# Splitting six weight pieces early and keeping them in DRAM, and making the similarities before the stage ends: one decoder layer on one Trainium2 core

## The chip, the cores and the metric

The kernel runs on one core of one Trainium2 chip. The metric is the device time of one execution in microseconds; the time given for a kernel is the median of several executions. All data are fp32, and every product of matrices is made of three passes over a "high" and a "low" part of each operand (float32r), so each weight and each activation is split into two parts before TensorE (PE) may use it.

## The reference

There are 32 batches of 128 positions by 1024 features. Three blocks follow each other, each with a residual and a layer norm:

```python
x = _layernorm(x + attention(x, wq, wk, wv, wo))       # 32 heads, 8 KV heads, rope, causal
x = _layernorm(x + xattn(x, ctx, weight))              # conv over 3 taps, inputs scaled by att
x = _layernorm(x + ffn(x, A, B, Wr, br))               # rank 16, 8 routed experts

def xattn(feature, embedding, weight):                 # embedding = ctx, [32, 128, 1024]
    # cosine of each column of the embedding with its left neighbour, itself, its right one
    sim = stack([cos(embedding, emb_l), cos(embedding, embedding), cos(embedding, emb_r)], 1)
    att = repeat(sim, C, axis=1)                       # [32, 3 * 128, 1024]
    out = einsum('bit,oi->bot', unfold3(feature) * att, weight)
```

With 128 positions the choice of key chunks leaves every key allowed, so the attention is a plain causal one. The three "similarities" of a batch depend on ctx alone.

## The kernel before, in words

**Stage one** (`part1`) runs steps t = 0 to 33. Step t projects batch t to q, k and v on PE (72 matmuls of 128x512, `project`, L483), and works on the attention of batch a = t-1 in eight chunks p = 0 to 7. A chunk goes from PE scores (`score`, L513) to DVE (`mask_min`), ACT (`exponent`, L769), DVE (`invert`, L629), POOL (`scale`, L915), DVE (`turn_p`, L637), and then by DMA (`move_p`, L322: ten small DMAs for each half of a batch) to `weigh` (L526). ACT copies the turned queries to SBUF (`copy_q`, L756) before `score` may run. The result goes to DRAM (`ot_dram`). Beside this each step squares and sums ctx (`square`, `neighbour`), stores the sums in DRAM (`cs_dram`), loads the next x (`load_x`, L297) and makes its high part at chunk 2 (`high_x`, L742).

Each engine has a written order of its own. The steps are a hardware loop with a few steps unrolled before it (LEAD) and after it (TAIL). Engines meet only by semaphores, and SP issues nearly all DMAs, in order, on one queue.

**Hand-over.** Stage two needs other weights in the same SBUF region: eight pieces of `wo`, `wb` and `wx`, ten "late pieces" in all. Each is loaded to a landing buffer, its high part is made by ACT (`high_later`, L796) and its low part by DVE (L644) or POOL (L928). Pieces 0 to 3 are made in step 31, the last projecting step, 4 to 8 in step 32 and `wb` in step 33. In step 32 PE has no projection; it does the output projection of batch 0 (`project_out`, L543) between the last scores, in step 33 that of half of batch 1. ACT also makes the high part of the attention output of batch 1 (`high_out(1)`, L827). The cosines come from the sums: `load_sums` and a lower bound (L725) in step 32, then a square root on ACT (L821), a reciprocal (L671) and four products on DVE, and the stores `store_sims` to `sim_dram` in step 33. SP then waits for these stores and loads half of the factors `att` of batch 0 (`start_att`, L985 and L990). At the end of the stage all engines meet at a barrier (L145).

**Stage two** (`part2`) has per step 48 matmuls of the output projection (L1197), 18 of the convolution (L1211), the low-rank block, and on DVE, ACT and POOL the products, norms and splits that feed them. Its first convolution multiplies `att` by the normalised x (`multiply`, L1380); DVE, POOL and ACT make the first norm (`average`, `invert_root`, `normalise1`, L1537). `turn_x2` (L1230) comes after the second norm of batch 0.

Of the kernel before, what the change touches and what calls it, by code (L numbers as in the profile page):

```python
# [23 lines left out]
P = 128  # L24
KT = D // P
HEADS, KVH, DH = 32, 8, 32
NU = 2
# [83 lines left out]
def build(nc, xT, x, ctx_in, wqkv, wo, wx, wa, wb, br, rope, mask, ident, out):  # L111
    ot_dram = nc.dram_tensor("ot_scratch", [B, P, D], F32, kind="Internal").ap()
    cs_dram = nc.dram_tensor("cs_scratch", [B, 2, D], F32, kind="Internal").ap()
    sim_dram = nc.dram_tensor("sim_scratch", [B, len(SIM_TABLE), D + SIM_PAD], F32, kind="Internal").ap()
    with ExitStack() as both:
# [28 lines left out]
            att, [both.enter_context(nc.semaphore(f"att_in{n}")) for n in range(2)])  # L144
        with ExitStack() as ctx:  # L145
            part1(nc, ctx, weights, raw, halves, wo_ps, handoff, xT, ctx_in, wqkv, wo, wx, wb,
                  rope, mask, ident, x, ot_dram, cs_dram, sim_dram)
# [4 lines left out]
def part1(nc, ctx, weights, raw, halves, wo_ps, handoff, xT, ctx_in, wqkv, wo, wx, wb,  # L152
          rope, mask, ident, x, ot_dram, cs_dram, sim_dram):
# [6 lines left out]
    def sem(name):  # L160
# [7 lines left out]
     added0, counted0, y0, stats0, xn1, kept, att, att_in) = handoff  # L168
# [72 lines left out]
    LEAD, TAIL = 4, 4  # L241
# [24 lines left out]
    LATER = KT + 2  # L266
    BY_POOL = (1, 3, 5, 8, 9)
    landing = [raw[:, 1], ctx_t[:, 0:D], raw[:, 0]]

    def lands(n):  # L270
        return n % 3 if n < KT + 1 else 1

    def later_parts(n):

        src = landing[lands(n)]
        if n < KT:
            return [(src, wo_sb[:, 0, n], wo_sb[:, 1, n])]
        if n == KT + 1:
            return [(src, wb_sb[:, 0], wb_sb[:, 1])]
        return [(src[:, 0:TAPS * P], wx_sb[:, 0], wx_sb[:, 1])]  # L280
# [7 lines left out]
    sqs, nbs, norm = nb[:, 0:QD + 1], nb[:, QD + 1:2 * QD + 1], nb[:, 2 * QD + 1:3 * QD + 2]  # L288
    own = rot1[:, 0, 0:QD]
    own_out = sem("own_out")  # L290
    right, ot_last = kept

    @block.sync
    def _(sp):
# [30 lines left out]
        def store_first_half(b):  # L325

            wait(sp, ot_read, after(b, NU, 1))
            sp.dma_start(ot_dram[b, :, 0:BANK], ot[:, 0]).then_inc(ot_out[0], 16)
# [6 lines left out]
        def load_later(n):  # L335
# [10 lines left out]
            dst, arrived = landing[lands(n)], later_in[lands(n)]  # L346
            if n < KT:
                sp.dma_start(dst, wo[:, n, :]).then_inc(arrived, 16)
            elif n == KT + 1:
                sp.dma_start(dst, wb).then_inc(arrived, 16)  # L350
            else:
                sp.dma_start(dst[:, 0:TAPS * P], wx).then_inc(arrived, 16)

        def load_o(t):

            wait(sp, x_lo, 2 * (B - 1 + t))
            if t == 1:
                later_done(sp, KT - 2)
# [4 lines left out]
        def load_third_o():  # L363

            later_done(sp, KT)
# [4 lines left out]
        def load_sums():  # L370

            sums = cs_dram[0, 0, 0:1]
            sp.wait_ge(cs_out, 16 * B)
            sp.wait_ge(summed, B)
            for dst, at, width in ((sqs, 0, QD + 1), (nbs, D, QD)):
                sp.dma_start(dst, bass.AP(tensor=sums.tensor, offset=sums.offset + at,
                                          ap=[[2 * D, B], [QD, 4], [1, width]])).then_inc(cs_in, 16)
# [8 lines left out]
        def store_sims():  # L386

            sp.wait_ge(sim_made, 1)
            for n in (3, 4):
                sp.dma_start(sim_row(sim_dram, n, 0), right).then_inc(sim_out, 16)  # L390
            sp.wait_ge(sim_made, 2)
            sp.dma_start(sim_row(sim_dram, 2, 0), own).then_inc(own_out, 16)
# [14 lines left out]
        def step(t, par):  # L407
# [19 lines left out]
            if at_step(t, LAST):  # L427
                store_sims()
                store_first_half(b)
                sp.wait_ge(own_out, 16)  # L430
                sp.wait_ge(sim_out, 16 * 6)
                start_att(sp, att, att_in, sim_dram, 0, 0)
            if at_step(t, B):
                load_later(7)
                load_later(8)
# [3 lines left out]
                sp.wait_ge(sq_done, B)  # L439
                sp.dma_start(xn1[:], x[1]).then_inc(xn_in[1], 16)  # L440
# [4 lines left out]
            if valid(t):  # L445
# [4 lines left out]
                             csum[:]).then_inc(cs_out, 16)  # L450
            if at_step(t, B - 1):
# [4 lines left out]
            if at_step(t, B):  # L456
                load_later(9)
                load_third_o()
            if at_step(t, B - 2):
# [3 lines left out]
            if at_step(t, B):  # L463
                store_later_half(b)
            if at_step(t, B - 1):
                load_later(4)

        steps(sp, step, 0, LAST, LEAD, TAIL)
        sp.wait_ge(ot_out[0], 16 * B)
        sp.wait_ge(ot_out[1], 16 * (B - 1))  # L470

    @block.tensor
    def _(pe):
# [58 lines left out]
        def project_out(t, n, k):  # L532
# [3 lines left out]
            if t == 0 and n == 0:  # L536
                later_done(pe, k)
# [53 lines left out]
    def _(dve):  # L591
# [76 lines left out]
        def invert_norms():  # L668

            dve.wait_ge(root, 1)  # L670
            dve.reciprocal(norm, norm).then_inc(cos_step, 1)  # L671

        def cosines():

            dve.wait_ge(cos_step, 1)
            dve.tensor_tensor(right, norm[:, 0:QD], norm[:, 1:QD + 1], ALU.mult).then_inc(cos_step, 1)
            dve.tensor_tensor(own, norm[:, 0:QD], norm[:, 0:QD], ALU.mult).then_inc(cos_step, 1)
            dve.wait_ge(cos_step, 2)
            dve.tensor_tensor(right, right, nbs, ALU.mult).then_inc(sim_made, 1)
            dve.wait_ge(cos_step, 3)  # L680
            dve.tensor_tensor(own, own, sqs[:, 0:QD], ALU.mult).then_inc(sim_made, 1)
# [10 lines left out]
        def step(t, par):  # L692
# [5 lines left out]
            for p in range(NC):  # L698
                if p == 0 and valid(a):
                    rotate(a, 1 - par, 2)  # L700
                if p == 0 and valid(b):
                    invert(b, NC - 1)
# [1059 lines left out]
```

## Time and profile before

| | |
|---|---|
| median of 3 executions | 1395.01 us (1394.53 to 1395.64) |
| the profiled execution | 1392.16 us, of which its span from the first to the last instruction is 1390.1 us |
| PE busy | 1355.7 us, 98% of the span |
| DVE, ACT, POOL busy | 79%, 67%, 70% |
| granted TensorE clock | 0.992 of full speed |
| HBM | 131.83 MB read, 34.47 MB written |

Stage one fills about the first 757 us of the span and stage two the rest. A matmul's busy time includes its pipeline, so a busy PE can still be held to less than its peak; idle time is what waits show directly. A late piece is a tile `weights<-raw` or `weights<-ctx_t` in the trace.

### The profile page before, as it was taken

What the parts mean: (1) busy time and instruction counts of PE and PEld (TensorE: products, weight loads), DVE (VectorE), ACT (ScalarE), POOL (GpSimd) and SP (SyncE); (2) the same over time, 40 slices, a digit from 0 to 9 for tenths busy, and PEclk for the clock granted to TensorE, in tenths of its full rate; (3) what the DMA queues carried; (4) which work ended last, traced back from release to release, by engine and by line L of the source; (5) the groups of instructions that cost most, each with busy time, mean ns of one, the idle gap of its engine ahead of it and who ended that gap; (6) DMA issues with size and microseconds to landing.
All of it is one profiled execution on the core that took longest, in us unless ns stands there. A gap on an engine that the chain in (4) does not pass through costs nothing. (4 is left out here: it accounts for less than half of the span.)

```text
span 1390.1 us, 32350 instructions
## 1 busy us (share of the span) xinstructions
PE 1355.7 (98%) x8306; PEld 1056.5 (76%) x8306; DVE 1095.9 (79%) x3873; ACT 927.2 (67%) x3262; POOL 979.0 (70%) x932
## 2 busy tenths in 40 slices
PE   8999999999999999999986999999999999999996
PEld 6777777777777777777764788888888888888884
DVE  6877787878778777878785688878887788877877
ACT  5887878878888887878785455545554455545544
POOL 4877777777777776777775677667776677767762
PEclk9999999999999999999998999999999999999999
DMA  7354545445453545445468866676665766666652
GB/s 266 100 160 116 159 116 161 121 146 149 121 161 115 165 115 152 132 134 159 131 201 242 185 159 166 157 174 153 161 156 164 172 152 165 156 169 157 161 122 76
DMA packets 109005, 213.03 MB, mean 153 GB/s; under 512 B 26656, under 2 KB 32288, under 8 KB 108960
## 3 DMA queue, kind: packets, MB, share of 16 engines
q1 hardware_dynamic: 108336, 211.46, 56.5%
q10 hardware_dynamic: 624, 1.05, 0.2%
q8 instruction: 18, 0.29, 0.1%
q14 instruction: 27, 0.22, 0.1%
HBM read 131.83 MB, written 34.47 MB: 120 GB/s over the span
## 5 line engine op out<-in xcount | busy, mean ns | idle before, releaser
L483 PE MATMUL wo_ps<-weights,halves 128*128 128x512 f32 x2304 | 569.7, 399 | 3.0 <-DVE weights L685 2.9
L483 PEld LDWEIGHTS wo_ps<-weights,halves 128*128 128x128 f32 x2304 | 421.5, 188 | 138.0 <-issue 53.3
L769 ACT ACTIVATE pexp<-sm,smin 128x128 f32<-128x128 f32 x1024 | 398.1, 391 | 100.6 <-DVE smin L622 99.7
L1197 PE MATMUL wo_ps<-weights,halves 128*128 128x512 f32 x1464 | 368.2, 399 | 4.3 <-PEq L145 4.3
L915 POOL TENSOR_TENSOR pn<-pexp,prec 128x512 f32<-128x512 f32 x256 | 266.7, 1047 | 98.5 <-DVE prec L629 98.5
L1667 POOL TENSOR_TENSOR prods<-prod,prods 128x512 fp32r<-128x512 f32 x186 | 251.6, 1360 | 119.9 <-ACT prods L1528 114.9
L1197 PEld LDWEIGHTS wo_ps<-weights,halves 128*128 128x128 f32 x1464 | 270.3, 189 | 62.6 <-issue 5.2
L622 DVE CUSTOM_DVE_ANT_0 sm<-s_ps,mask_t 128x128 f32<-128x128 f32 x1024 | 231.9, 282 | 26.1 <-PE s_ps L513 20.9
L1528 ACT CAST prods<-prod 128x512 fp32r<-128x512 f32 x189 | 117.1, 620 | 181.0 <-DVE prod L1380 146.7
L769 ACT ACTIVATION_READ_ACCUMULATOR pexp<-sm,smin 128x1 f32 x1024 | 193.0, 189 | 0.0
L1380 DVE TENSOR_TENSOR prod<-att,x 128x512 f32<-128x512 f32 x189 | 185.1, 993 | 9.5 <-DMA att<-sim_scratch 7.2
L637 DVE STREAM_TRANSPOSE blocks<-pn 128x512 f32<-128x512 f32 x256 | 178.0, 695 | 6.5 <-POOL pn L915 6.2
L1211 PE MATMUL conv_ps<-prods,weights 128*128 128x512 f32 x567 | 144.2, 396 | 1.7 <-POOL prods L1667 1.2
L910 POOL TENSOR_TENSOR xn<-rot,y 128x512 f32<-128x512 f32 x64 | 83.8, 1310 | 68.5 <-DVE y L609 68.3
L1356 DVE BATCH_NORM_STATS2 stats<-y 128x6 f32<-128x512 f32 x188 | 127.3, 690 | 4.4
L1211 PEld LDWEIGHTS conv_ps<-prods,weights 128*128 128x128 f32 x567 | 105.9, 188 | 28.6 <-POOL prods L1667 2.6
L1661 POOL TENSOR_TENSOR moments<-moments,power 128x1 f32<-128x1 f32 x96 | 76.7, 799 | 62.7 <-DVE moments L1365 62.7
L629 DVE RECIPROCAL prec<-psum_row 128x4 f32<-128x4 f32 x256 | 44.9, 175 | 67.5 <-ACT pexp L769 67.5
L889 POOL TENSOR_TENSOR halves<-raw,halves 128x512 fp32r<-128x512 f32 x62 | 79.7, 1287 | 25.1 <-ACT halves L742 25.1
L604 DVE TENSOR_TENSOR rot<-wo_ps,rope_t 128x512 f32<-128x512 f32 (+1 forms) x96 | 56.7, 591 | 44.0 <-PE wo_ps L483 42.1
L1653 POOL TENSOR_TENSOR halves<-raw,halves 128x512 fp32r<-128x512 f32 x60 | 90.6, 1510 | 0.0
L622 DVE DVE_READ_ACCUMULATOR2_ANT smin<- 128x1 f32 x1024 | 85.1, 83 | 0.0
(130 smaller groups left out, 1645.8 us busy)
## 6 DMA issues: line engine op xcount, KB each, us to landing
att<-sim_scratch SPq DMA_DIRECT2D x192, 252.0 KB
pt<-blocks SPq DMA_DIRECT2D x636, 64.0 KB, 2.0
ctx_t<-in_ctx SPq DMA_DIRECT2D x32, 576.0 KB, 5.1
raw<-in_xT SPq DMA_DIRECT2D x32, 512.0 KB, 3.8
xn<-in_x SPq DMA_DIRECT2D x32, 512.0 KB, 7.6
ot_scratch<-ot SPq DMA_DIRECT2D x63, 256.0 KB, 2.1
raw<-ot_scratch SPq DMA_DIRECT2D x31, 512.0 KB, 6.8
out<-late SPq DMA_DIRECT2D x31, 512.0 KB, 6.2
```

Source lines behind the costliest of these rows:

```text
L483: mm = pe.matmul(qkv_ps[(par + g) % 2][:], xs[:, par, xl, k], w_sb[:, wl, g, k], start=(k == 0 and n == 0), stop=(k == KT - 1 and n == 2))
L622: ins = dve.tensor_tensor_reduce(sm[:, c % 2, i * P:(i + 1) * P], s_ps[i][:, j * P:(j + 1) * P], mask_t[:], 1.0, 3e38, ALU.add, ALU.min, s ...
L637: dve.transpose(blocks[:, u, :, j], pn[:, c % 2].rearrange("p (i b k) -> p b i k", i=NI, b=QB)).then_inc(turned, 1)
L769: ins = nc.scalar.activation(pexp[:, c % 2, i * P:(i + 1) * P], sm[:, c % 2, i * P:(i + 1) * P], ACT.Exp, bias=smin[:, c % 2, i:i + 1], sc ...
L915: pool.tensor_tensor(pn[:, c % 2].rearrange("p (i s) -> p i s", i=NI), pexp[:, c % 2].rearrange("p (i s) -> p i s", i=NI), prec[:, c % 2]. ...
L1197: mm = pe.matmul(wo_ps[n][:], os_t[:, par, ol, k], wo_sb[:, wl, k, n * BANK:(n + 1) * BANK], start=(k == 0 and m == 0), stop=(k == KT - 1 ...
L1211: mm = pe.matmul(conv_ps[h][:], wx_sb[:, wl, k], prods_home(t, m, xl), start=(k == 0 and n == 0), stop=(k == TAPS - 1 and n == 2))
L1356: dve.bn_stats(stats[own][:, half], src).then_inc(counted[n], 1)
L1380: dve.tensor_tensor(prod_home(t, m), att[:, k, h * BANK:(h + 1) * BANK], x1[:, par, h * BANK + k:h * BANK + k + BANK], ALU.mult).then_inc( ...
L1528: nc.scalar.copy(prods_home(t, m, 0), prod_home(t, m)).then_inc(prod_hi, 1)
L1653: pool.tensor_tensor(lo, oraw[:, par, cols], hi.bitcast(F32), ALU.subtract).then_inc(o_lo, 1)
L1667: pool.tensor_tensor(prods[:, m % PB, 1], prod[:, m % PB], prods[:, m % PB, 0].bitcast(F32), ALU.subtract).then_inc(prod_lo, 1)
```

## The change

Six of the ten late pieces (wo pieces 4 to 7, `wb` and `wx`) are no longer made in steps 32 and 33. In steps 2 to 7 SP loads one of them a step into `att`, which stage one does not otherwise use; ACT makes the high part at chunk 5 and POOL the low part (128x1024) at chunk 6, and at the start of the next step SP stores both parts to a new DRAM buffer. They come back to their places in the weight region as 1 MB DMAs: pieces 0 and 1 at the end of step 31, 2 and 3 at the start of step 32, `wb` and `wx` later in step 32. Only pieces 0 to 3 of `wo` are still made at the end.

The similarities of batches 0 to 15 are made in steps 20 to 25 with 64 partitions (each small operation at chunk 5), and `att` of batch 0 is loaded whole in steps 26 to 29, one of its four DMAs at the end of each step, ahead of the next step's `load_x`. Those of batches 16 to 31 are made at the end. The first norm of batch 0 is made before the barrier, and also the two parts of the attention output of batch 2. `high_out(1)` moves from chunk 6 to chunk 5 of step 32. `xn1` is loaded at the end of step 31. The unrolled ends grow from 4 and 4 steps to 10 and 14.

```diff
-    LEAD, TAIL = 4, 4
+    LEAD, TAIL = 10, 14
+    FIRST = B // 2
+    EARLY = B - 12
...
-    LATER = KT + 2
-    BY_POOL = (1, 3, 5, 8, 9)
+    LATER = KT // 2
+    BY_POOL = (1, 3)
+    SPLIT_AT = 2
+    SPLITS = KT // 2 + 2
...
+        def load_source(n):
+            wait(sp, split_lo, n)
+            sp.dma_start(split_parts(n)[0], split_source(n)).then_inc(split_src, 16)
+        def store_split(n):
+            sp.wait_ge(split_lo, n + 1)
+            both = split_parts(n)[1]
+            sp.dma_start(split_dram[n, :, :, 0:both.shape[2]], both).then_inc(split_out, 16)
+        def load_split(n):
+            sp.wait_ge(split_out, 16 * SPLITS)
+            sp.wait_ge(qkv_done, after(B - 1, NG, 2 if n < SPLITS - 2 else NG))
+            home = split_home(n).bitcast(F32)
+            sp.dma_start(home, split_dram[n, :, :, 0:home.shape[2]]).then_inc(split_in[n], 16)
...  (SP's step: at its start)
+            if at_step(t, EARLY):
+                load_sums(False)
+            for n in range(SPLITS):
+                if at_step(t, SPLIT_AT + n + 1):
+                    store_split(n)
+                if at_step(t, SPLIT_AT + n):
+                    load_source(n)
             if at_step(t, B):
-                load_sums()
-                load_later(5)
-                load_later(6)
+                load_sums(True)
+                load_split(2)
+                load_split(3)
...
             if at_step(t, LAST):
-                store_sims()
                 store_first_half(b)
-                sp.wait_ge(own_out, 16)
-                sp.wait_ge(sim_out, 16 * 6)
-                start_att(sp, att, att_in, sim_dram, 0, 0)
+                store_sims(True)
             if at_step(t, B):
-                load_later(7)
-                load_later(8)
                 load_o(1)
...  (and at its end)
+            for n in range(len(RUNS) + 1):
+                if at_step(t, EARLY + 6 + n):
+                    ...
+                    start_att(sp, att, att_in[0], sim_dram, 0, 0, D, (n,))
             if at_step(t, B - 1):
-                load_later(4)
+                load_split(0)
+                load_split(1)
+                sp.dma_start(xn1[:], x[1]).then_inc(xn_in[1], 16)
...  (ACT)
+        def high_split(n):
+            src, both = split_parts(n)
+            act.wait_ge(split_src, 16 * (n + 1))
+            wait(act, split_out, 16 * n)
+            nc.scalar.copy(both[:, 0].bitcast(F32R), src).then_inc(split_hi, 1)
...  (DVE)
             if at_step(t, LAST):
-                invert_norms()
-                cosines()
                 add_first(1)
+                average_first()
+                invert_norms(True, 0, HALF_QD)
+                invert_norms(True, HALF_QD, QD + 1)
+                pair_norms(True)
+                cosines(True)
+                low_third_out()
```

## Rows read from the trace of the kernel before

**Rows 1.** Busy time by stretch: us, PE, PEld, DVE, ACT, POOL, clock, DMA share, GB/s.
```profile
0.00:20.00 20.00, 15.76 (x47) 10.72 (x48) 11.18 (x12) 12.81 (x12) 3.55 (x9) 0.91 0.92 344
...
40.00:620.00 580.00, 579.32 (x4239) 430.76 (x4240) 463.98 (x2301) 476.66 (x2259) 429.64 (x394) 1.00 0.48 139
...
720.00:740.00 20.00, 15.56 (x126) 9.88 (x127) 17.58 (x74) 16.16 (x63) 12.96 (x9) 0.91 0.80 248
740.00:760.00 20.00, 12.67 (x55) 7.69 (x54) 9.72 (x28) 8.91 (x26) 8.89 (x7) 0.91 0.91 259
760.00:800.00 40.00, 37.21 (x159) 29.66 (x160) 25.13 (x51) 18.63 (x26) 26.50 (x26) 0.92 0.90 189
```

**Rows 2.** Timeline of PE, hand-over: start, duration, [idle before it <- what ended it].
```profile
746.63 1.94 PE L526 MATMUL pv_ps<-pt,v_t 128*32 128x512 f32 x8 [3.17 <-DMA pt<-blocks]
...
755.24 1.06 PE L526 MATMUL pv_ps<-pt,v_t 128*32 128x512 f32 x8 [0.47 <-DMA pt<-blocks]
760.62 7.88 PE L1197 MATMUL wo_ps<-weights,halves 128*128 128x512 f32 x21 [4.31 <-PEq L145]
...
777.61 5.64 PE L1197 MATMUL wo_ps<-weights,halves 128*128 128x512 f32 x24
784.36 1.06 PE L1230 MATMUL ffn_ps<-id_t,late 128*128 128x128 f32 x8 [1.11 <-ACT late L1547]
```

**Rows 3.** Timeline of SP's queue, steps 32 and 33.
```profile
736.19 0.33 SPq L361 DMA_DIRECT2D raw<-ot_scratch  x1
...
750.97 1.53 SPq L390 DMA_DIRECT2D sim_scratch<-kept  x2
...
759.05 0.77 SPq L990 DMA_DIRECT2D att<-sim_scratch  x1
```

**Rows 4.** Timelines of ACT and DVE, steps 32 and 33.
```profile
742.03 1.04 ACT L827 CAST halves<-raw 128x1024 fp32r<-128x1024 f32 x1
...
745.11 1.28 ACT L821 ACT_TABLE_LOAD   x1
746.40 0.42 ACT L821 ACTIVATE nb<-nb 128x257 f32<-128x257 f32 x1
...
756.37 0.59 ACT L778 COPY kept<-pv_ps 128x512 f32<-128x512 f32 x1 [2.87 <-PE pv_ps L526]
...
747.09 1.72 DVE L671 RECIPROCAL nb<-nb 128x257 f32<-128x257 f32 x1
```

**Rows 5.** Timelines of SP, ACT, POOL and PE in one steady step.
```profile
653.92 0.36 SPq L297 DMA_DIRECT2D raw<-in_xT  x1
...
646.20 0.40 ACT L769 ACTIVATE pexp<-sm,smin 128x128 f32<-128x128 f32 x1 [2.13 <-DVE smin L622]
...
655.57 0.39 ACT L769 ACTIVATE pexp<-sm,smin 128x128 f32<-128x128 f32 x1
...
657.96 1.05 ACT L742 CAST halves<-raw 128x1024 fp32r<-128x1024 f32 x1 [0.75 <-DMA raw<-in_xT]
...
660.47 0.56 ACT L756 COPY qt<-turn_ps 128x512 f32<-128x512 f32 x1
...
653.46 1.05 POOL L915 TENSOR_TENSOR pn<-pexp,prec 128x512 f32<-128x512 f32 x1
...
661.79 1.17 PE L513 MATMUL s_ps<-kt,qt 32*128 32x128 f32 x32
```

**Rows 6.** Timelines of POOL and DVE: low parts of late pieces.
```profile
719.85 3.37 POOL L928 TENSOR_TENSOR weights<-raw,weights 128x1024 fp32r<-128x1024 f32 x1
...
731.63 2.42 POOL L928 TENSOR_TENSOR weights<-raw,weights 128x1024 fp32r<-128x1024 f32 x1
...
719.29 1.68 DVE L644 TENSOR_TENSOR weights<-raw,weights 128x1024 fp32r<-128x1024 f32 x1
```

**Rows 7.** Issue to landing of v_t<-v_new (L309): step 28, then step 30.
```profile
DMA to landing us min/median/max: 5.4/5.4/5.4
...
DMA to landing us min/median/max: 7.5/7.5/7.5
```

More of the change, by code:

```diff
@@ L287, in part1, with sim_parts @@
     QD = D // 4
-    sqs, nbs, norm = nb[:, 0:QD + 1], nb[:, QD + 1:2 * QD + 1], nb[:, 2 * QD + 1:3 * QD + 2]
-    own = rot1[:, 0, 0:QD]
-    own_out = sem("own_out")
+    HALF_QD = QD // 2
     right, ot_last = kept
+    ot_first = xn0[:, BANK:D]
+    def sim_parts(late):
+        rows = slice(4 * FIRST, P) if late else slice(0, 4 * FIRST)
+        flat = nb if late else att[:].rearrange("p k d -> p (k d)")
+        sums, mults, norm = (flat[rows, n * (QD + 1):n * (QD + 1) + width]
+                             for n, width in enumerate((QD + 1, QD, QD + 1)))
+        pair = (right[rows, :], xn0[rows, 0:QD]) if late else (
+            flat[rows, 3 * (QD + 1):3 * (QD + 1) + QD], flat[rows, 4 * (QD + 1):4 * (QD + 1) + QD])
+        return sums, mults, norm, *pair
     @block.sync
@@ L384, in store_zeros, with store_sims @@
                              allow_slow_non_contiguous=True).then_inc(sim_out, 16)
[L386 to L392, printed above, removed]
+        def store_sims(late):
+            first, count = (FIRST, B - FIRST) if late else (0, FIRST)
+            to_right, to_own = sim_parts(late)[3:5]
+            sp.wait_ge(sim_made, 2 * late + 1)
+            for n, shift in ((0, 1), (1, 1), (3, 0), (4, 0)):
+                sp.dma_start(sim_row(sim_dram, n, shift, first, count), to_right).then_inc(sim_out, 16)
+            sp.wait_ge(sim_made, 2 * late + 2)
+            sp.dma_start(sim_row(sim_dram, 2, 0, first, count), to_own).then_inc(own_out, 16)
         sp.dma_start(xraw[:, 0], xT[0]).then_inc(x_in[0], 16)
@@ L666, in add_first, with low_third_out @@
             dve.bn_stats(stats0[:, half], y0[:, cols]).then_inc(counted0, 1)
-        def invert_norms():
-            dve.wait_ge(root, 1)
-            dve.reciprocal(norm, norm).then_inc(cos_step, 1)
[L673 to L681, printed above, removed]
+        def low_third_out():
+            dve.wait_ge(o_hi, 3)
+            hi, lo = (halves[:, 0, part].rearrange("p t s -> p (t s)") for part in range(2))
+            dve.tensor_tensor(lo, raw[:, 0], hi.bitcast(F32), ALU.subtract).then_inc(o_lo, 2)
@@ L775, in read_ot @@
             wait(act, pv_done, after(a, NU, u + 1))
-            if not (at_step(a, B - 1) and u == 1):
-                wait(act, ot_out[u], after(a, 16, 0))
-            nc.scalar.copy(ot_last if at_step(a, B - 1) and u == 1 else ot[:, u], pv_ps[:]).then_inc(ot_read, 1)
+            if at_step(a, B - 1):
+                if u == 0:
+                    act.wait_ge(added0, 2)
+                nc.scalar.copy((ot_first, ot_last)[u], pv_ps[:]).then_inc(ot_read, 1)
+                return
+            wait(act, ot_out[u], after(a, 16, 0))
+            nc.scalar.copy(ot[:, u], pv_ps[:]).then_inc(ot_read, 1)
         def move_last_row():
@@ L993, in sim_row, with start_att @@
-def sim_row(sim_dram, n, shift):
-    row = sim_dram[0, n, 0:1]
+def start_att(sp, att, arrived, sim_dram, t, lo, hi, parts=range(len(RUNS) + 1)):
+    cols, width = slice(lo, hi), hi - lo
+    for n in parts:
+        if n < len(RUNS):
+            (first, last), row = RUNS[n], (0, 2, 3)[n]
+            sp.dma_start(att[first:last, :, cols],
+                         sim_dram[t, row, cols].unsqueeze(0).unsqueeze(0).broadcast_to([last - first, TAPS, width])
+                         ).then_inc(arrived, 16)
+        else:
+            rows = sim_dram[t, 0:TAPS, cols]
+            both_edges = bass.AP(tensor=rows.tensor, offset=rows.offset,
+                                 ap=[[2 * (D + SIM_PAD), 2]] + [list(d) for d in rows.ap])
+            sp.dma_start(att[EDGES[0]:EDGES[1] + 1:EDGES[1] - EDGES[0], :, cols], both_edges).then_inc(arrived, 16)
@@ L1077, in part2 @@
     held = sem("held2")
[L1078 removed]
+    shifted = [first_steps[3]] + [sem(f"shifted{n}") for n in range(1, 3)]
     stored = [sem("stored0"), sem("stored1")]
@@ L1439, in step @@
                 low_lt(z)
-            if valid(c):
+            if valid(c) and not at_step(c, 0):
                 average(c, 0)
```

235 lines of the change are left out of this document (143 added, 92 removed).

## The prediction

> **What bounds the kernel now.** I read the busy time by stretch first [rows 1]. From 40 to 620 us PE is busy 579.32 of 580 us: in the steady part of stage one nothing can be won by unloading DVE, ACT or POOL, and everything that makes PE wait is lost. From 720 to 760 us PE is busy for only 28.2 of 40 us, and from 760 to 800 for 37.2 of 40. The hand-over is the only place with something to win, and most of the change's work is there. ACT is busy 82% and POOL 74% in the steady part; what the change puts there has to fit in their holes.
>
> Then PE's own timeline [rows 2]. In step 33 PE waits 3.17 us, and later 0.47 us, for the DMAs that bring the last probabilities; then comes the barrier, 4.31 us; then 21 matmuls take 7.88 us where the same kind runs at 24 in 5.64 us a little later (so 21 would take 4.9): the granted clock is at its lower level, 1.2 instead of 2.4 GHz, for part of them. The last wait is 1.11 us for the second norm of batch 0. After this PE is full again, so any time gained up to 784.36 us is kept.
>
> Third, who comes last to the barrier. PE ends at 755.24 + 1.06 = 756.3 us, ACT's last copy at 756.37 + 0.59 = 757.0 [rows 4], and SP's last issue, the loads of `att`, at 759.05 + 0.77 = 759.8 [rows 3]. PE starts 0.8 us after that. SP sets the barrier, not PE.
>
> **The barrier.** The change takes the `att` loads and the wait for the sims' stores off SP's end. What SP has left is the first-half store and five stores of sims, at 1.53 / 2 = 0.77 us each for four and some 0.6 for the fifth [rows 3]. They need the cosines. The last transposes end as the old reciprocal begins, at 747.1 [rows 4]; from there DVE does the second half of the first sum with its statistics (some 1.4 us, an estimate), the average (0.5), two reciprocals (1.72 together) and four small products (1.6, an estimate from their size): 752.3. SP can then end at 752.3 + 3.1 + 0.6 = 756.0. `low_third_out` is a 128x1024 subtract, 1.7 us on DVE [rows 6], done by 754.0. So ACT's copy at 757.0 is now last, and PE starts at about 757.0 + 0.8 = 757.8 instead of 760.6: **-2.9 us**, if the last probabilities land when they did.
>
> **Do they land earlier?** ACT loses five casts in step 32 (four at 1.04, one at 0.5), 4.7 us [rows 4]; DVE and POOL lose as much. One would hope for up to 4.7 us. But `high_out(1)` now stands one chunk earlier, and ACT blocks there until the attention output of batch 1 has landed. SP can issue that load some 3 us earlier than at 736.19 [rows 3], since it no longer waits for the splits of two pieces. Ahead of it are, from 720.7 on, four split pieces of 1.05 MB, `xn1` 0.52, sums 0.26, v 0.13, the ten DMAs of one half of the probabilities, 0.66 in all, and one store of 0.26: 6.0 MB. The stretch with the largest DMAs moved 344 GB/s at a share of 0.92, so 374 at a full share [rows 1]: 16 us, and 1.4 for the load itself, with some 2 us around them: 740.2. After the cast follow two chunks (four exps of 0.39 each, 1.6) and one copy (0.5): the table load would start at 744.9, against 745.11 [rows 4]. So ACT's gain is eaten by the queue, and the end of step 33 stays where it was. Bounds: at 420 GB/s, 1.9 us less; at 259, the rate of 740 to 760 us [rows 1], the load lands after 747, and the end is 5 to 6 us later. I take **0**.
>
> **After the barrier.** `att` is in SBUF, the first norm is made, and ACT and POOL have no split of batch 2 in front of them. Convolutions still come at fixed places in PE's order, behind 21 matmuls. Nothing is won if these are as slow as now and the chain to `turn_x2` keeps its length; at most the 2.9 us of the clock and the 1.11 us of the wait, 4.0 [rows 2]. PE was at the low level after the idle times of 3.17 and 4.31 us: 1.94 us for eight matmuls of L526 against 1.06. The gap at the barrier shrinks to 1.4 us, but before the last `weigh` a gap of about 3 us opens, because the projection ahead of it ends earlier while the DMAs do not. So the lower half is likelier: **-1.7 us**.
>
> **Steps 2 to 7.** ACT's cast is 1.04 us; at chunk 5 ACT has a hole of 2.13 us [rows 5], and the piece, queued behind x, ctx and one 1 MB store, lands some 9 us after the step's first load, before ACT is there. POOL's low part is 2.42 us, or 3.37 where DVE read two SBUF operands at the same time (its own low part, 719.29) [rows 6]; DVE has no such instruction in these steps, so 2.42. It delays `scale` of the last chunk from 653.46 to 655.9; the second exp chunk of the next batch, which waits for it, starts at 656.9 instead of 655.57 and ends at 658.4, where `high_x` starts at 657.96 because of its DMA: 0.45 late. `copy_q` ends at 661.5 instead of 661.0, and `score` is due at 661.79 [rows 5]: hidden, with 0.3 us left. At 3.37 it would be 0.7 a step. **+0.1.** Two more DMAs a step on SP cost under 1 us of issue, in front of loads with 9 us of slack. Should that cover be gone, six steps times the 0.7 would be 4 us.
>
> **Steps 20 to 25.** The early root makes ACT load a table twice: 1.28 + 0.42 + 1.28 = 2.98 us [rows 4] in the same 2.13 us hole; 0.85 late, most of which the margin before the next `score` takes: **+0.3**. The DVE pieces (0.4 to 0.9 us each) fit before the rotation for which it waits. SP's five stores, 3.7 us, stand in its idle time before `move_p`.
> The Trainium skill, "ScalarE: Activation LUTs", section "What ACT_TABLE_LOAD costs", puts a switch at some 2.66 us, drain included: 5.7 us here, and +3.0 instead of +0.3. The trace differs: the root starts 0.01 us after the load ends.
>
> **Steps 26 to 29.** Three DMAs of 504 KB for `att` (42 partitions, three rows of 4 KB each) stand right ahead of `load_x`; the fourth is small. ACT already waits 0.75 us for x in each step, so all delay of x goes through. The queue is in order: with a load of 512 KB put before it in step 30, v_t landed in 7.5 us instead of 5.4 [rows 7]. So x comes later by 0.4 of issue and by 1.0 (504 KB at full rate, half hidden by the store ahead) to 2.1 us. From `copy_q`'s end at 661.03 to `score` at 661.79 there are 0.76 us [rows 5]. PE waits 0.6 to 1.7 us a step; the next step hangs on PE's time, so it repeats: 1.9 to 5.2 in three steps. I take 0.93 each, **+2.8 us**.
>
> **Sum.** -2.9 + 0 - 1.7 + 0.1 + 0.3 + 2.8 = -1.4 us on the profiled execution of 1392.16 us (2.1 us of which lie outside its span): 1390.8. The median is 2.85 us above that execution, so 1393.6. About 2.8 us, 0.2%, is what a measurement of this kernel can tell from no change. The gain at the barrier is half given back in steps 26 to 28.
>
> **Rivals.** (1) *It pays.* x is held up by no more than the margin (PE waits 0.3 a step, not 0.93), and PE starts stage two at 2.4 GHz: -2.9 - 4.0 + 0.1 + 0.3 + 0.9 = -5.6, **1389.4**; with a faster queue another 1.9. For it: the `att` DMAs may overlap x's; against it: rows 7 and the gap before `weigh`. 0.37.
> (2) *The queue is flooded* in step 32, the rival on the other side. At 259 GB/s the 6 MB need 23 us, and ACT's cast of batch 1 starts at 748 instead of 742.03; exps, transposes, last probabilities and the barrier follow, 5 to 6 us later: -1.4 + 5.5 = +4.1, **1399.1**. It turns to a loss once that load lands after about 743.5. For it: small DMAs lie between the large ones; against it: all of the large ones have rows of 4 KB, as in the stretch with 344 GB/s. 0.12.
> (3) *`att` is slow to load*: while such loads ran, the queues moved 189 GB/s at a share of 0.90 [rows 1], where 504 KB take 2.7 us. PE then waits 2.2 us in each of three steps, 3.9 more than in the sum: -1.4 + 3.9 = +2.5, **1397.5**; with the 0.4 us that the rows leave open it is beyond 0.2%, and I count it as slower. 0.10.
> (4) *The table switch costs more*: if each of the two loads in step 20 held ACT for its own length again (1.28) [rows 4], `copy_q` would come 2.6 us later and PE wait all of it: -1.4 + 2.6 = +1.2, **1396.2**. The root directly behind its load speaks against it. 0.03. The Trainium skill's "ScalarE: Activation LUTs" is the page by whose figure it would be so.
> (5) The forecast, within 0.2% of before: 0.38.
>
> **How the numbers follow.** Faster 0.37 (rival 1), same 0.41 (forecast and rival 4), slower 0.22 (rivals 2 and 3). The likeliest case's own range is 1392.2 to 1396.5. The range for 8 in 10 leaves out the best of rival 1 and the worst of rival 2: 1388.5 to 1399.
>
> **What would show it.** The wait of PE at the barrier should fall from 4.3 to about 1.4 us, and its first matmul of stage two come at about 761 (757.8 plus 3.2 of delays in stage one). `high_x` should wait for x 2 to 3 us, not 0.75, in steps 27 to 29, each with a new wait of PE for `copy_q` of about 1 us, and none in steps 2 to 7. The table load at the end of step 32 should keep its distance to the step's start, with ACT waiting at `high_out(1)` for its DMA. The forecast is wrong if that wait is absent (then rival 1 with the faster queue), if it is over 5 us (rival 2), or if PE shows waits for `copy_q` in the six splitting steps.

## The result, and the profile after

The changed kernel takes **1414.79 us** (median of 4 executions, 1411.68 to 1417.62) against 1395.33 for the kernel before beside it: ratio 1.0136, 95% interval 1.0115 to 1.0157. It is 19.5 us slower, where 1393.6 was forecast and 1399 was the upper end. The profiled execution took 1411.68 us; its span is 1409.9 us against 1390.1.

Busy time by stretch, changed kernel (us, PE, PEld, DVE, ACT, POOL, clock, DMA share, GB/s):

```profile
40.00:620.00 580.00, 572.78 (x4172) 424.60 (x4171) 461.60 (x2284) 478.53 (x2247) 437.30 (x395) 1.00 0.55 152
620.00:720.00 100.00, 91.98 (x654) 67.83 (x653) 71.37 (x359) 73.58 (x351) 66.34 (x61) 0.98 0.56 146
720.00:740.00 20.00, 17.69 (x112) 13.13 (x114) 15.67 (x67) 16.36 (x57) 15.25 (x13) 0.91 0.60 184
740.00:760.00 20.00, 12.47 (x117) 8.41 (x111) 12.14 (x73) 11.61 (x55) 10.72 (x9) 0.91 1.01 331
```

From 40 to 620 us PE was idle for 0.68 us before [rows 1] and is idle for 7.2 now; in the next 100 us it is idle for 8.0, against 2.8 before. The time went in the steady part, where nothing of PE's own work was touched. PE's waits over the whole changed kernel (total us, times, longest):

```profile
PE s_ps L576 <- ACT qt L860: 13.5, 13, 3.8
PE pv_ps L589 <- DMA pt<-blocks: 12.9, 3, 8.4
...
PE wo_ps L1328 <- PEq L151: 0.9, 1, 0.9
```

Before, these three were 4.2 us (3 times), 3.6 and 4.3. `score` waits for `copy_q` thirteen times, the last probabilities cost three times as much, and the barrier, as forecast, almost nothing. PE's timeline in the hand-over shows the last two and the low clock behind them:

```profile
761.17 1.93 PE L589 MATMUL pv_ps<-pt,v_t 128*32 128x512 f32 x8 [8.41 <-DMA pt<-blocks]
769.49 1.06 PE L589 MATMUL pv_ps<-pt,v_t 128*32 128x512 f32 x8 [1.02 <-DMA pt<-blocks]
779.66 1.19 PE L589 MATMUL pv_ps<-pt,v_t 128*32 128x512 f32 x8 [3.42 <-DMA pt<-blocks]
781.80 7.60 PE L1328 MATMUL wo_ps<-weights,halves 128*128 128x512 f32 x21 [0.94 <-PEq L151]
...
804.54 1.06 PE L1361 MATMUL ffn_ps<-id_t,late 128*128 128x128 f32 x8 [1.10 <-ACT late L1680]
```

Set against [rows 2]: 3.17 has become 8.41 us, the barrier's 4.31 has become 0.94, and 21 matmuls take 7.60 instead of 7.88.

To place the rest I noted, in PE's timeline, when the first transposition of `turn_k` starts in each step (steps are numbered by SP; `turn_k(31)` is the last). The table gives these starts, then the first matmul of stage two, `turn_x2`, and the span, for the kernels of this study. A steady step is 22.24 us long.

| us | before | changed | unrolled only | att moved | queue order | x early | all three | half pieces |
|---|---|---|---|---|---|---|---|---|
| `turn_k(0)` | 23.69 | 25.64 | 24.12 | | | 24.34 | 24.17 | |
| `turn_k(9)` | 221.71 | 226.71 | 223.01 | | | 221.48 | 221.38 | |
| `turn_k(26)` | 600.04 | 608.87 | 605.58 | | | 600.95 | 600.85 | |
| `turn_k(31)` | 711.34 | 730.09 | 717.76 | 718.25 | 731.35 | 712.45 | 712.35 | 714.05 |
| stage two | 760.62 | 781.80 | 767.87 | 771.21 | 780.50 | 763.12 | 763.14 | 760.18 |
| `turn_x2` | 784.36 | 804.54 | 791.50 | 794.13 | 802.26 | 785.29 | 784.92 | 781.82 |
| span | 1390.1 | 1409.9 | 1397.6 | 1399.5 | 1407.6 | 1390.6 | 1390.3 | 1387.1 |

The changed kernel's 19.8 us of span, read down the column: 1.95 before `turn_k(0)` (the first x landed later and a POOL subtract took 3.5 instead of 2.5 us; this stretch varies from 23.7 to 25.6 us over the runs, whatever the edit); 6.9 up to `turn_k(26)`; 9.9 from there to `turn_k(31)`, the steps with the `att` loads (11.2 and 13.4 in the traces of runs 4 and 3 below, which load `att` at the same place); 2.4 in the hand-over (51.71 us from `turn_k(31)` to stage two instead of 49.28); -1.0 up to `turn_x2`; -0.4 after.

One of the `att` steps shows the whole chain, in the timelines of SP, ACT and PE:

```profile
659.61 7.29 SPq L355 DMA_DIRECT2D pt<-blocks  x10
666.94 0.58 SPq L363 DMA_DIRECT2D ot_scratch<-ot  x1
667.57 0.44 SPq L1114 DMA_DIRECT2D att<-sim_scratch  x1
668.05 0.39 SPq L330 DMA_DIRECT2D raw<-in_xT  x1
...
675.31 1.04 ACT L846 CAST halves<-raw 128x1024 fp32r<-128x1024 f32 x1 [5.48 <-DMA raw<-in_xT]
...
677.81 0.56 ACT L860 COPY qt<-turn_ps 128x512 f32<-128x512 f32 x1
...
678.43 2.09 PE L576 MATMUL s_ps<-kt,qt 32*128 32x128 f32 x32 [3.77 <-ACT qt L860]
```

The load of x stands behind ten small DMAs, a store and an `att` load. It lands 7.2 us after its issue (3.8 is the median in the kernel before); ACT sits idle for 5.48 us, `copy_q` is queued behind the cast, `score` comes 3.77 us late and then runs at the lower granted clock, 1.2 instead of 2.4 GHz (32 matmuls in 2.09 instead of 1.17 us). In the four steps PE waits 1.98, 1.67, 3.77 and 0.60 us.

The hand-over, from SP's queue in steps 31 and 32:

```profile
739.45 1.26 SPq L399 DMA_DIRECT2D weights<-split_scratch  x2
740.76 0.60 SPq L528 DMA_DIRECT2D xn<-in_x  x1
741.45 1.23 SPq L425 DMA_DIRECT2D nb<-cs_scratch  x2
742.78 1.28 SPq L399 DMA_DIRECT2D weights<-split_scratch  x2
...
752.42 1.60 SPq L408 DMA_DIRECT2D raw<-ot_scratch  x1
```

The attention output of batch 1 (L408) lands 11.7 us after its issue, and in ACT's timeline `high_out(1)` waits for it, with the exps, the table load and the last copies behind it:

```profile
764.19 1.04 ACT L939 CAST halves<-raw 128x1024 fp32r<-128x1024 f32 x1 [7.97 <-DMA raw<-ot_scratch]
...
768.82 1.28 ACT L930 ACT_TABLE_LOAD   x1
...
780.90 0.58 ACT L883 COPY kept<-pv_ps 128x512 f32<-128x512 f32 x1 [4.27 <-PE pv_ps L589]
```

### The profile page after: what moved, and what is told of

It is laid out like the page before. It is cut to its first block and busy times, and to the rows that moved or that the text cites. A ratio compares the mean times of both kernels' runs of the same rounds, so it can differ in the third digit from the quotient of the medians.

```text
span 1409.9 us, 31220 instructions
## 1 busy us (share of the span) xinstructions
PE 1360.6 (97%) x8306; PEld 1059.6 (75%) x8306; DVE 1096.1 (78%) x3878; ACT 929.1 (66%) x3265; POOL 985.2 (70%) x934
## 5 line engine op out<-in xcount | busy, mean ns | idle before, releaser
L1001 POOL TENSOR_TENSOR halves<-raw,halves 128x512 fp32r<-128x512 f32 x62 | 80.7, 1302 | 45.6 <-ACT halves L846 45.5
L576 PEld LDWEIGHTS s_ps<-kt,qt 32*128 32x128 f32 x2048 | 63.8, 188 | 39.0 <-ACT qt L860 20.9
L576 PE MATMUL s_ps<-kt,qt 32*128 32x128 f32 x2048 | 76.0, 285 | 14.7 <-ACT qt L860 13.5
```

The costliest lines, as they stand in the source:

```text
L576: mm = pe.matmul(s_ps[i][:, j * P:(j + 1) * P], qt[rows, u, j * P:(j + 1) * P], kt[rows, par, u * P:(u + 1) * P], start=True, stop=True, t ...
```

## Experiments

My first theory after the result was that four things had been added: the longer straight-line ends of the loops, the `att` loads ahead of x, the flooded queue of step 32, and perhaps the split work of ACT and POOL in steps 2 to 7. Rivals were that one of them was all of it, and that the split work was what cost in the early steps. Medians are given beside the ratio to the kernel before in the same session.

**1. Unrolling alone.** The kernel before, one line changed:

```diff
-    LEAD, TAIL = 4, 4
+    LEAD, TAIL = 10, 14
```

> The kernel before with only the unrolled ends grown from 4 and 4 steps to 10 and 14. The changed kernel lost 18.8 us in stage one (turn_k of step 31 at 730.09 us instead of 711.34) before the hand-over began. Theory A (the losses are x arriving late behind new DMAs): unrolling costs nothing, 1394 to 1397 us, no new wait of PE in steps 0 to 29. Theory B (more straight-line code, so more instruction fetches beside the data, slows everything a little; in the changed kernel x lands in 4.3 to 4.9 us even in steps without new DMAs, against 3.8): 2 to 6 us slower, x landing at 4.3 us or more.

Measured 1400.93 us, ratio 1.0043 (1.0027 to 1.0060): some 6 us for no new work, and x lands 4.4 us (median) after its issue instead of 3.8. That is theory B. Where the time goes, in the timelines of SP, ACT and PE:

```profile
516.52 7.89 SPq L322 DMA_DIRECT2D pt<-blocks  x10
524.45 0.59 SPq L328 DMA_DIRECT2D ot_scratch<-ot  x1
525.08 0.46 SPq L297 DMA_DIRECT2D raw<-in_xT  x1
...
529.88 1.05 ACT L742 CAST halves<-raw 128x1024 fp32r<-128x1024 f32 x1 [3.13 <-DMA raw<-in_xT]
...
533.00 1.17 PE L513 MATMUL s_ps<-kt,qt 32*128 32x128 f32 x32 [1.41 <-ACT qt L756]
...
360.12 6.25 SPq L322 DMA_DIRECT2D pt<-blocks  x10
```

Once the loop has gone round once, SP issues the ten DMAs of the probabilities in about 6.2 us, each time. In the unrolled steps, and in the loop's first pass, one issue in every step or two takes 0.9 to 1.9 instead of 0.6 us, and x, which comes behind, is late by more than the 0.76 us that `copy_q` has in hand [rows 5]. From 30 to 700 us there are 22 issues of 0.9 us or more in this trace, 31 in the changed kernel's and 6 before, none of them in a later pass of the loop. PE's waits for `copy_q` sum to 5.2 us up to 715 us (9 times), against 0.6 before.

**2. The `att` loads moved** behind the store of the context sums, some 10 us ahead of the next x:

```diff
+            for n in range(len(RUNS) + 1):
+                if at_step(t, EARLY + 6 + n):
+                    ...
+                    start_att(sp, att, att_in[0], sim_dram, 0, 0, D, (n,))
             if at_step(t, B - 1):
                 load_later(2)
```

(the same lines go from the step's end)

> The changed kernel with one move: in steps 26 to 29 the DMA for att is issued behind the store of the sums, some 10 us before the next x, instead of right ahead of load_x. Theory A (att in front of x costs the 10 us of steps 27 to 30): 9 to 10 us faster than the changed kernel, 1404 to 1406 us, and steps 27 to 30 at 22.3 us each. Rival (the load from sim_dram itself is slow and disturbs wherever it stands): less than 4 us faster, 1411 us or more.

Measured 1401.17 us, ratio 1.0048 (1.0033 to 1.0063): 12 to 14 us faster than the changed kernel, more than theory A's 9 to 10, and the four steps are 22.31 to 22.44 us long. In the traces the steps from `turn_k(26)` to `turn_k(31)` give 9.5 us of it (111.7 instead of 121.2); the rest I can't place. The `att` loads cost what they do by where they stand.

**3. The queue of step 32** in another order:

```diff
                 load_sums(True)
-                load_split(2)
-                load_split(3)
...
                 load_o(1)
                 wait(sp, q_turned, NU * B)
                 sp.dma_start(xn0[:], x[0]).then_inc(xn_in[0], 16)
+                load_split(2)
+                load_split(3)
+                sp.wait_ge(sq_done, B)
+                sp.dma_start(xn1[:], x[1]).then_inc(xn_in[1], 16)
```

(`xn1` is no longer loaded at the end of step 31)

> The changed kernel with another order of the large loads in steps 31 and 32: xn1, and pieces 2 and 3, behind the first ten probability DMAs of step 32, the load of the attention output of batch 1 and xn0. Theory A (the flood: 4.7 MB ahead of the probabilities make PE wait 8.4 us and ACT 8.0 us): these two waits fall below 3 us and the hand-over shortens by 3 to 6 us, 1409 to 1412 us. Rival (the bytes count, not their order; a later transfer then waits as long): the same time within 1.5 us, with the wait at another DMA.

Measured 1409.4 us, ratio 1.0107 (1.0089 to 1.0124): about 4 to 5 us faster, though this interval and the changed kernel's (1.0115 to 1.0157) overlap. From `turn_k(31)` to stage two it takes 49.15 us instead of 51.71. The waits for the last probabilities fall from 12.9 to 2.9 us, but PE waits 3.9 us for a split piece instead. The time is in theory A's range; that the wait moves to another DMA is what the rival said.

**4. The split work left out.** Pieces 1 to 5 are neither loaded, cast nor subtracted in steps 3 to 7; their stores stay, with the data of piece 0. The computation is changed by that.

```diff
-            sp.wait_ge(split_lo, n + 1)
+            sp.wait_ge(split_lo, 1)
-                    if p == 5 and at_step(t, SPLIT_AT + n):
+                    if n == 0 and p == 5 and at_step(t, SPLIT_AT + n):
                         high_split(n)
```

(and the same condition before `load_source` and `low_split`)

> The changed kernel with the loads, casts and subtracts of pieces 1 to 5 left out in steps 3 to 7 (their parts are those of piece 0, so part of the computation is left out); the six 1 MB stores stay. The changed kernel loses 3.4 us between steps 2 and 9. Theory A (POOL's 2.4 us delays the next exp and with it copy_q): 2.5 to 3.5 us faster than the changed kernel, 1411 to 1412.5 us, and no wait of PE in steps 4 to 8. Rival (the 1 MB stores make x late): the waits stay, within 1 us of the changed kernel.

Measured 1411.9 us, ratio 1.0120 (1.0103 to 1.0136). The median is in theory A's range, but the interval overlaps the changed kernel's, and the trace speaks for the rival: from `turn_k(0)` to `turn_k(9)` it takes 200.5 us against 201.1, and steps of 22.9 to 23.4 us are still there. By the trace the split work of ACT and POOL costs next to nothing; runs 5 and 6 settle it.

**5 to 8. One edit against all the losses of stage one.** If all of it is x coming late, x has only to be asked for earlier: its buffer is free from the step before on.

```diff
             if valid(t + 1):
-                if not at_step(t, 0) and not at_step(t, 1) and not at_step(t, 2):
-                    load_x(t + 1, 1 - par)
                 load_ctx(t + 1)
...
                 wait(sp, pv_done, after(a - 1, NU, 1))
-            if at_step(t, 1):
-                load_x(3, 1)
+            if valid(t + 2) and not at_step(t, 0):
+                load_x(t + 2, par)
```

It was made in the unrolled kernel of run 1, in the changed kernel, and in the changed kernel with edits 2 and 3, which also ran without it.

> The kernel before with its ends unrolled to 10 and 14 steps (1400.93 us, 5.9 over before), and in every step the load of x for the step after the next now stands before the store of the context sums, some 10 us earlier than at the start of the next step. Theory A: unrolling costs because single DMA issues of SP take 1.2 to 1.9 us in straight-line code, and x, issued last of the chain, comes later than the 0.76 us that copy_q has in hand; with x some 10 us early the same slow issues stay but PE's waits for copy_q in unrolled steps vanish, and the time is 1395 to 1396.5. Rival B: what costs is the slow issues in front of the ten DMAs of the probabilities, or slow instructions of PE itself; then x early changes nothing, 1400 to 1401.5, or worse, since x's 512 KB are now in front of the probabilities.

> The changed kernel with nothing different but the loads of x, issued some 10 us earlier as in the run above; the loads of att in steps 26 to 29 stand where the change has them. Theory A: att costs its 10 to 13 us through x alone, so steps 27 to 30 fall from 24.34, 24.03, 27.59 and 22.96 us to about 22.3, and with the losses of the other unrolled steps gone too the time is 1414.8 - 10 - 5 = about 1399 to 1401 us. Rival B: att's DMAs delay the context, v and the probabilities just as much; then PE waits there instead and the time stays above 1406 us.

> The changed kernel with both earlier edits: the att loads behind the store of the context sums (alone 1401.17 us) and, in step 32, xn1 and two split pieces behind the attention output of batch 1 (alone 1409.4 us). Theory A: the two faults are separate and add: 1401.2 - 5.4 = 1395.8 us. Rival B: they share their loss, because the later start of step 32 let the queue run empty or the split pieces are missed by the output projection (3.9 us of wait in the run of that edit alone) whatever comes before: 1398 to 1400 us.

> The run above and x early in every step as well: the change with its three faults mended. Theory A: 1395.8 less about 5 us of unrolled steps = 1391 us, so that the gain at the barrier is seen in the time. Rival B: with 1400 from the run above and x early worth nothing: 1398 to 1400 us.

| kernel | without x early | with x early |
|---|---|---|
| before, unrolled | 1.0043 (1.0027 to 1.0060) | 1394.37 us, 1.0004 (0.9994 to 1.0013) |
| changed | 1.0136 (1.0115 to 1.0157) | 1393.92 us, 0.9998 (0.9988 to 1.0008) |
| changed, att and queue moved | 1399.4 us, 1.0031 (1.0019 to 1.0044) | 1392.07 us, 0.9985 (0.9975 to 0.9995) |

Theory A holds for these three runs (5, 6 and 8), for 5 and 8 to about 1 us; in run 6 I had still left 5 us too much, since more than the unrolled steps' and the `att` loads' losses came back. The slow issues are all still there (22 in run 5, 33 in run 6, counted as in run 1), and so is each `att` load. The same step of run 6, on SP and ACT:

```profile
647.91 7.33 SPq L355 DMA_DIRECT2D pt<-blocks  x10
655.28 0.58 SPq L363 DMA_DIRECT2D ot_scratch<-ot  x1
655.90 0.45 SPq L1112 DMA_DIRECT2D att<-sim_scratch  x1
656.45 0.34 SPq L336 DMA_DIRECT2D ctx_t<-in_ctx  x1
...
658.03 1.03 ACT L844 CAST halves<-raw 128x1024 fp32r<-128x1024 f32 x1
```

The ten issues again take over 7 us and `att` is ahead of ctx, but ACT casts x at its turn, with no wait, and the steps are 22.30 us long. PE's one wait from 200 to 700 us is then this, against 9.2 us for `copy_q` in the changed kernel:

```profile
PE turn_ps L563 <- ACT kt L863: 0.8, 1, 0.8
```

It stands in step 20, the early root. Run 7's time is in rival B's range (1399.4, where A gave 1395.8), but the trace does not bear out B's cause. From `turn_k(31)` to `turn_x2` it takes 72.8 us instead of run 2's 75.9, so the new queue gains 3.1 us there, as it gained 3.5 in run 3 (70.9 against 74.5); the wait for a split piece, 4.1 us, was in run 3 too (3.9). What is longer is `turn_k(0)` to `turn_k(9)`, 202.5 us against run 2's 200.2, where the two kernels do the same: x coming late costs more in one execution than in another. By the ratios the repairs would add to 1.0048 - 0.0029 = 1.0019, the edge of run 7's interval. Whether they add is open.

**9. The control.** The kernel before with x early, the same diff.

> The kernel before with nothing different but x loaded some 10 us earlier: the control for the runs with x early (1394.4, 1393.9 and 1392.1 us). Theory A: before loses to late x only what its few unrolled steps lose; PE's steps of over 22.24 us there sum to some 0.3 to 0.7 us, so it gains at most that, 1394.3 to 1395 us, and the run with all three edits stays 1.5 to 2.5 us faster. Rival B: x early is worth 1.5 us or more in any kernel, 1392 to 1393 us, and then the change is worth nothing even when mended.

Measured 1393.05 us, ratio 0.9987 (0.9978 to 0.9996), 1.8 us. That is B's forecast. The trace shows 0.5 us of it (`turn_k(31)` at 711.38 in spite of a start 0.56 later, all steps of 22.86 and 22.35 us gone); for the rest I have no row, and the interval allows it to be noise. So the mended change (0.9985) is not shown to be faster than the kernel before with the same mend.

**10. Another order of step 32:** all three edits, and

```diff
+                load_split(2)
...
                 load_o(1)
+                load_split(3)
                 wait(sp, q_turned, NU * B)
                 sp.dma_start(xn0[:], x[0]).then_inc(xn_in[0], 16)
-                load_split(2)
-                load_split(3)
```

> The run with all three edits (1392.07 us), with the queue of step 32 in another order: one split piece where the change has it, then the attention output of batch 1, then the second split piece, xn0 and xn1. There PE waited 4.6 us for the second or first split piece and 3.0 us for the last probabilities. Theory A: the piece that PE waits for lands some 3 us earlier and the attention output at most 2 us later, so that the two waits together fall by 2 to 4 us: 1388.5 to 1390.5. Rival B: the bytes ahead of the last probabilities are the same, and one wait takes over what the other gives: 1391.5 to 1393.

Measured 1392.37 us, ratio 0.9979 (0.9969 to 0.9989); run 8 was at 0.9985. By the time that is B; the two intervals overlap. It is the fastest version that computes everything, 2 to 3 us better than the kernel before, and not told apart from run 9. Its profiled execution was its slowest (1396.76 us), with no wait for a split piece and 12.5 us of waits for the probabilities, so that trace shows one wait taking over from the other, but not in a typical execution: the hand-over differs by some us from one to the next.

**11 and 12. Whose straight-line code is it?** Again the kernel before; in 11 all engines but SP have the long ends, in 12 only SP has them:

```diff
         steps(sp, step, 0, LAST, 4, 4)      # run 11, with LEAD, TAIL = 10, 14
         steps(sp, step, 0, LAST, 10, 14)    # run 12, with LEAD, TAIL = 4, 4
```

> The kernel before with the program ends of PE, DVE, ACT and POOL unrolled to 10 and 14 steps, and SP's left at 4 and 4. With all five unrolled it took 1400.93 us, 5.9 over before. Theory A: the slow issues of SP come from SP's own straight-line program; looped, it issues evenly and the loss is gone, 1395 to 1396 us. Rival B: they come from the fetching of all engines' instructions, which shares the queues with the data; then most of the loss stays, 1398.5 to 1401 us.

> The reverse: the kernel before with only SP's program unrolled to 10 and 14 steps. Theory A: nearly the whole loss comes back, 1399 to 1401 us, with PE's waits for copy_q in unrolled steps. Rival B: under 1.5 us of it, 1395 to 1396.5 us.

Measured 1400.92 us, ratio 1.0036 (1.0024 to 1.0048), for run 11, and 1396.32 us, ratio 1.0002 (0.9993 to 1.0011), for run 12. Theory A, which I held, falls: SP's slow issues come although SP's own program is looped (17 of them; the group of ten at 516.02 us takes 7.48 us), and are no more than before when only SP is unrolled (7, against 6). PE's waits for `copy_q` up to 715 us are 6.1 us in run 11 and 2.2 in run 12. What goes with the slow issues is the instruction traffic of the others, in the table of DMA queues up to 720 us (packets, MB, share), run 11 and then run 12:

```profile
q8 instruction: 30, 0.49, 0.3%
q14 instruction: 45, 0.37, 0.2%
```

```profile
q8 instruction: 9, 0.15, 0.1%
q14 instruction: 20, 0.16, 0.1%
```

Run 1 has 30 and 49 packets there, before has 9 and 16. The Trainium skill, "DMA: Bandwidth & Descriptors", section "Queues, rings and completion order", has queue row 14 as the runtime's own, for refills among others; the trace's name for q14, "instruction", fits that. That the packets themselves hold up SP's issue, and not something else in those engines' programs, is argued, not shown.

**13 and 14. Where the barrier's 3 us went.** With x early the changed kernel waits 0.9 us at the barrier and still is no faster. The pieces kept as two parts are 1.05 MB each (`wx` is smaller) where the unsplit ones were 0.5. In these runs each is loaded home with its high part alone, so the low parts of six pieces are left out of the computation:

```diff
-            sp.dma_start(home, split_dram[n, :, :, 0:home.shape[2]])
+            sp.dma_start(home[:, 0], split_dram[n, :, 0, 0:home.shape[2]])
```

> The changed kernel with x early (1393.92 us), but each of the six pieces is loaded home with its high part alone, 0.5 MB in place of 1.05; the low parts are left out of the output projection's and the later weights, so part of the computation is changed. There PE waited 12.0 us for the last probabilities and only 0.9 at the barrier. Theory A: the gain at the barrier is eaten by the bytes: the pieces kept as two parts are twice as many bytes as the unsplit ones, in the queue that carries the last probabilities; with 3.1 MB less (some 9 us at 340 GB/s, of which those ahead of the attention output count) the wait falls by 3 to 5 us, 1389 to 1391 us. Rival B: it is the chain of casts, exps and small DMAs, not bytes, and the time stays within 1 us, 1393 to 1395.

> The same halving in the run with all edits and the order of step 32 changed (1392.37 us). Theory A: 1388 to 1390 us, no wait of PE for a split piece, and 4 us or less for the last probabilities. Rival B: 1391.5 to 1393 us.

Measured 1388.92 us, ratio 0.9955 (0.9940 to 0.9970), against 0.9998 in run 6, and 1387.18 us, ratio 0.9942 (0.9925 to 0.9958), against 0.9979 in run 10: 6 and 5 us faster, a little more than theory A said of either. Busy time by stretch, run 6 and then run 13:

```profile
720.00:740.00 20.00, 14.75 (x120) 9.85 (x119) 14.50 (x75) 13.89 (x61) 12.79 (x10) 0.92 0.94 310
740.00:760.00 20.00, 13.33 (x55) 8.30 (x55) 11.22 (x28) 7.95 (x22) 5.33 (x6) 0.83 0.99 296
```

```profile
720.00:740.00 20.00, 15.03 (x131) 10.35 (x135) 14.98 (x76) 15.80 (x70) 13.93 (x11) 0.99 0.91 255
740.00:760.00 20.00, 14.56 (x63) 7.96 (x55) 11.06 (x28) 8.53 (x23) 5.36 (x6) 0.84 0.80 236
```

From 720 to 760 us, 20 x (310 + 296) = 12.1 MB against 9.8 MB, and 10.1 before [rows 1]. PE's waits for the last probabilities in the hand-over, again run 6 and then run 13:

```profile
PE pv_ps L587 <- DMA pt<-blocks: 12.0, 3, 7.7
```

```profile
PE pv_ps L587 <- DMA pt<-blocks: 7.4, 2, 4.6
```

From `turn_k(31)` to stage two it takes 46.13 instead of 50.67 us; before it was 49.28, so the 3 us of the barrier are there once the bytes are gone. Run 14 also takes 46.13 us. Theory A holds in both for the time; in run 14 it was wrong on the waits, which are 1.8 us for a split piece (none forecast) and 5.9 for the last probabilities (4 or less).

## Why the prediction was wrong, step by step

Three terms failed: the straight-line ends had none, the `att` steps cost 9.9 us instead of 2.8, and the last probabilities 5.8 instead of 0.

- **The barrier, -2.9: right.** SP is no longer last; ACT's copy of `kept` ends at 781.48 and PE starts 0.32 us later. The wait is 0.94 us (1.4 forecast), 3.4 less than before.
- **The last probabilities, 0: wrong by 5.8 us**, the hand-over's +2.4 with the barrier's -3.4 taken off. This is rival 2, which had 0.12. The doubled pieces were in my 6.0 MB, and SP reached the load of batch 1's attention output about when I said (22.3 us after `turn_k(31)`, 21.9 forecast). What was too small was the time that the bytes take. I let them move at 374 GB/s, the opening stretch's rate scaled to a full share, and had the load landed 19.5 us after the first piece was issued (720.7 to 740.2). It took 24.7 us (739.45 to 764.1): the queues moved 313 GB/s at a share of 1.01, and 7.7 MB instead of the 6.0 and the load's 0.5, since what is issued behind the load moves beside it (a DMA of the probabilities issued at 756.11 landed at 763.05, ahead of the load). That is 5.2 of the 5.8 us. My own sign for this rival was a wait of over 5 us at `high_out(1)`; it is 7.97. Runs 13 and 14 show that the bytes are the cause: with half of the pieces' bytes gone the hand-over is 4.5 us shorter. Some 0.8 us may be the straight-line ends, as in run 1 (50.11 us against 49.28). The 420 GB/s of my better bound stand on no row: none of the stretches that I read moved more than 350 or so.
- **After the barrier, -1.7: about the size, in part by luck.** It was -1.0, and -1.6 in run 6 (22.17 us from stage two to `turn_x2` against 23.74). The clock gave 0.3 us of it, 21 matmuls in 7.60 us, and 7.05 in run 6, instead of 7.88; but the wait at `turn_x2`, the other term, stayed (1.10 and 1.13 us against 1.11), and what helped instead were waits for the convolution's products, 0.67 us instead of 1.06.
- **Steps 2 to 7, +0.1: right in what it priced.** Run 4 takes the work away and nothing changes; in run 6 it is there and the steps are 22.30 us, as in run 5, which has none of it. The waits for `copy_q` that I named as the sign against me did appear, by another cause.
- **Steps 20 to 25, +0.3: too small.** Step 20 is 0.9 us longer in run 6 (23.22 against 22.31 us in run 5). The two table loads and the root held ACT from 465.77 to 468.79 as worked out, but what was queued behind them was `copy_k`, not `copy_q`, with less in hand. The Trainium skill, "ScalarE: Activation LUTs", section "What ACT_TABLE_LOAD costs", adds a drain of about 1.38 us to each load. This trace shows none: each load takes 1.28 us, the first starts 0.02 us after the copy ahead of it, the root 0.02 us after the first load, the second load 0.02 us after the root, and the next exp 0.01 us after that.
- **Steps 26 to 29, +2.8: the right mechanism, wrong in size, 9.9 us.** Of this 0.9 us is in run 1 too. x landed up to 7.2 us after its issue instead of 4.0 [rows 5], 3.2 more where I had allowed 2.1, and it was issued later as well, by SP's slow issues; one wait of 3.77 us then brought the low clock. I had taken 0.93 a step from the middle of 0.6 to 1.7, with an issue that was always even.
- **The longer straight-line ends: no term at all.** I took `LEAD, TAIL = 10, 14` to be the place where the edits stand, and gave it nothing. Alone it costs 6 us (run 1), 5.1 of them before `turn_k(26)`, the greater part of the 6.9 us lost there. This is the step that failed outright: a term put at nothing without a reason. The trace before held a sign of it, which I did not look for: all six slow issues were in unrolled steps or the loop's first pass, and so was its one long step (22.86 us, from `turn_k(4)` to `turn_k(5)`).

The three losses of stage one were one: a load with 0.76 us in hand, issued last behind a dozen others. Moving that load took back 19 of the 20 us, with every added piece of work still in place (run 6); up to `turn_k(31)`, 16.3 of the 16.8 us lost after `turn_k(0)` (688.1 us against 704.5, and 687.7 before).

## What to carry to other kernels

Ask of each load not how busy the queue is but how long the engine that waits for it can still wait, and issue the one with the least in hand first; where its buffer is free a step earlier, that cost nothing here. Unrolling loop ends to place edits is itself an edit: compare it alone. Work moved to an earlier time and parked in DRAM comes back as bytes; here they came when the queue was fullest, so count them there, at a rate read from such a stretch.

## What the hardware showed that I had not expected

- With PE, DVE, ACT and POOL running straight-line code, single DMA issues of SP take 0.9 to 1.9 us instead of 0.6 (17 in run 11, with SP itself looped); while all engines are in their loops, after the first pass, none does. The instruction queues carry 30 and 45 packets then instead of 9 and 16.
- The load of x, 512 KB, lands 3.8 us after its issue in the kernel before (median) and 4.0 to 4.8 in the unrolled steps of run 1; behind one more load of 504 KB it was 6.2 to 7.2. In run 12, where only SP is unrolled and the slow issues are gone, it is still 4.3 (median).
- Which wait PE shows in the hand-over (probabilities, a weight piece, the barrier) follows the order of the queue. The length of the hand-over follows the bytes: 49.1 to 53.2 us in the eight traces with the whole pieces, 46.13 in both with half of them.

Left open: by what the instruction traffic delays SP, and what the similarities moved early would be worth without the pieces parked in DRAM, which wasn't tried.
